# Branch hints on eleven loops, a larger DMA share of the transposes, and a clearing pass in smaller pieces, in a one-core attention and deformable-convolution kernel

## The reference

```python
# layer 0: group norm (32 groups), q/k/v, full attention over the 4096 pixels, projection, residual
h = group_norm(x, norm_w, norm_b)
qkv = einsum('bchw,dc->bdhw', h, qkv_w) + qkv_b
q, k, v = split(qkv.reshape(B, 3 * C, N), 3, axis=1)
attn = softmax(einsum('bcn,bcm->bnm', q, k) * C ** -0.5, axis=-1)
out = einsum('bnm,bcm->bcn', attn, v).reshape(B, C, H, W)
x = x + einsum('bchw,dc->bdhw', out, proj_w) + proj_b
# layer 1: conv 3x3, batch norm, relu; offsets by a second conv; deformable 3x3 conv; batch norm; residual, relu
out = relu(batchnorm(conv2d(x, w1), g1, b1))
offsets = conv2d(out, w_off) + b_off          # 18 offsets a pixel
out = batchnorm(deform_conv(out, offsets, w2), g2, b2)
return relu(out + x)
```

## Time and profile before

| | |
|---|---|
| three timed runs | 2494.53, 2494.78, 2497.68 us, median 2494.78 |
| the profiled execution | 2493.83 us, of which 2491.7 us lie between the first and the last instruction (the span) |
| busy: PE, DVE, ACT, POOL | 2315.7, 1855.8, 1795.1, 1310.9 us (93, 74, 72, 53% of the span) |
| attention, up to | about 1597 us |
| conv1, up to | about 1739 us |
| offset stage, up to | about 1872 us |
| sampling stage, up to | about 2440 us |

### The profile page before, as it was taken

How to read it: one execution, slowest core, us unless ns; L and a number is a source line. 1 busy time by engine, 2 the same in 40 slices (tenths; PEclk the granted TensorE clock), 3 DMA queues, 4 the chain that set the end, 5 groups by cost and what they waited for, 6 DMA issues and landing times.

```text
span 2491.7 us, 73903 instructions
## 1 busy us (share of the span) xinstructions
PE 2315.7 (93%) x27053; PEld 1877.2 (75%) x27053; DVE 1855.8 (74%) x3901; ACT 1795.1 (72%) x2963; POOL 1310.9 (53%) x1067
## 2 busy tenths in 40 slices
PE   5999999999999999999999999799877999899992
PEld 3777777777777777777777777588447999899992
DVE  6778777778877777877777777587666877777875
ACT  5778888878888888888888888532556766666754
POOL 4557545555545555544555555663116665556650
PEclk9999999999999999999999999899898999999996
DMA  3878887778787877877777777771224433333336
GB/s 108 166 144 147 141 162 140 147 149 146 145 159 133 150 145 145 150 129 129 149 147 146 148 146 148 192 235 59 66 71 133 124 113 113 111 111 117 115 95 270
DMA packets 917462, 345.25 MB, mean 139 GB/s; under 512 B 844256, under 2 KB 904160, under 8 KB 909024
## 3 DMA queue, kind: packets, MB, share of 16 engines
q1 hardware_dynamic: 917216, 341.87, 63.6%
HBM read 98.76 MB, written 41.68 MB: 56 GB/s over the span
## 4 chain that ended last, share of the span: by engine, by line
PE 75%; issue 9%; POOL 7%; DVE 4%; DMA 3%; ACT 1%; SPq 1%; POOLq 0%; DVEq 0%; ACTq 0%
PE psum L1041 14%; PE psum L1042 14%; PE psum L1043 14%; POOL probs_split L363 7%; PE psum L1080 7%; PE psum L1082 7%; PE psum L1081 7%; PE psum L1222 5%; PE psum L1066 3%; DMA probsT_dma<-probs_split 1%; PE psum L1195 1%; DMA final<-x_scratch 1%; DVE padded_hi L946 0%; PE psum L1120 0%; PE psum L1203 0%
## 5 line engine op out<-in xcount | busy, mean ns | idle before, releaser
L363 POOL TENSOR_TENSOR probs_split<-probs,probs_split 128x768 f16<-128x768 f32 x512 | 841.8, 1644 | 697.0 <-ACT probs_split L512 696.8
L711 DVE TENSOR_REDUCE neg_max<-psum 128x1 f32<-128x1024 f32 x512 | 626.6, 1224 | 333.0 <-PE psum L1043 332.8
L509 ACT ACTIVATE probs<-psum,exp_bias 128x1024 f32<-128x1024 f32 x512 | 570.2, 1114 | 220.2 <-DVE exp_bias L713 215.6
L1080 PE MATMUL psum<-vT_hi,probsT_dma 128*128 128x129 f16 x3072 | 549.6, 221 | 4.1 <-DMA probsT_dma<-probs_split 4.1
L1082 PE MATMUL psum<-vT_hi,probsT_dma 128*128 128x129 f16 x3072 | 549.5, 219 | 0.0
L1081 PE MATMUL psum<-vT_lo,probsT_dma 128*128 128x128 f16 x3072 | 549.4, 218 | 0.0
L512 ACT ACTIVATE probs_split<-probs 128x768 f16<-128x768 f32 x512 | 431.7, 843 | 22.8 <-ACT probs L509 1.0
L455 POOL TENSOR_TENSOR interp<-row_hats,col_hats 128x360 f32<-128x360 f32 x384 | 294.4, 795 | 219.6 <-PE psum L1222 214.7
L1041 PE MATMUL psum<-k_hi,q_hi 128*128 128x512 f16 x1024 | 387.8, 379 | 3.9 <-DVE q_lo L827 2.4
L1042 PE MATMUL psum<-k_lo,q_hi 128*128 128x512 f16 x1024 | 388.1, 379 | 0.0
L1043 PE MATMUL psum<-k_hi,q_lo 128*128 128x512 f16 x1024 | 388.1, 379 | 0.0
(11 more groups left out here) (181 smaller groups left out, 5532.1 us busy)
## 6 DMA issues: line engine op xcount, KB each, us to landing
xt_windows<-xt_scratch SPq DMA_DIRECT2D x192, 320.0 KB
xt_scratch<-zeros_f SPq DMA_DIRECT2D x28, 576.0 KB, 4.4
probsT_dma<-probs_split SPq DMA_TRANSPOSE x512, 3.7
x_residual<-x SPq DMA_DIRECT2D x128, 64.0 KB, 2.6
x_scratch<-x_out SPq DMA_DIRECT2D x128, 64.0 KB, 2.4
x_rows<-x_scratch SPq DMA_DIRECT2D x32, 256.0 KB, 3.4
xt_scratch<-xt_stage SPq DMA_DIRECT2D x128, 64.0 KB
final<-x_scratch SPq DMA_DIRECT2D x16, 512.0 KB, 10.7
```

What stands on the lines that cost most here:

```text
L363: po.tensor_tensor(PH[:, j, 1, :], P[:, j, 0:DW], PH[:, j, 0, :], ALU.subtract).then_inc(s["pl"], 1)
L509: act.activation(P[:, j, :], sc, ACT.Exp, bias=NB[:, par, j:j + 1]).then_inc(s["exp"], 1)
L711: ve.tensor_reduce(NM[:, par, j:j + 1], sc, AX.X, ALU.max, negate=True).then_inc(s["mx"], 1)
L1080: pe.matmul(dst, th, Vh[:, p, v, 0:129], start=n == 0, stop=False)
```

## The change

Three parts, made together.

1. **Loop hints, and clearing by blocks.** Eleven of the loops of layer 1 become `repeat(...)`, which is the same `Fori` with `hint_back_edge=True`: the first instruction of every iteration is a branch prefetch hint for the branch that closes the loop. These are conv1, the offset stage and the loop over halves on PE, DVE and ACT, and conv1 and the loop over halves on POOL. The attention loops, the loop over passes (one pass here) and SP's loops stay as they are. POOL clears `Y` with 32 memsets of 512 columns, each after ACT has read that block, in place of four of 4096.
2. **Key tiles.** In chunks 1 and 3 of each tile seven key tiles go by DMA and one by PE; in chunks 0 and 2 it stays at six and two. Each chunk has its own buffers.
3. **Late constants.** The columns from 454 on are loaded into a tile `CL` of layer 1's memory, by a DMA that SP issues after the conv1 loop, in place of the load at the start. The operation that makes `offset_high` from them moves from ahead of the first batch norm to behind it, and waits for the load.

```diff
-DT = 6
-DW = 128 * DT
+DT = (6, 7, 6, 7)
...
-        CN = sb_in(ctx, "constants", [128, K_ALL], F32)
+        CN = sb_in(ctx, "constants", [128, K_LO], F32)
...
+        CL = sb_in(l1, "late_constants", [128, K_ALL - K_LO], F32)
...
+        def repeat(eng, start, end):
+            return nc.Fori(start, end, engines=[eng.engine], hint_back_edge=True)
...
+            sp.dma_start(CL[:, :], consts[:, K_LO:K_ALL]).then_inc(s_kl, 16)
             sp.wait_ge(s_zf, 16 * 28)
...
-                    po.tensor_tensor(PH[:, j, 1, :], P[:, j, 0:DW], PH[:, j, 0, :], ALU.subtract).then_inc(s["pl"], 1)
+                    po.tensor_tensor(PH[j][:, 1, :], P[:, j, 0:128 * DT[j]], PH[j][:, 0, :], ALU.subtract).then_inc(s["pl"], 1)
...
-            for b in range(B):
-                after(po, "hA", (b + 1) * NCH)
-                po.memset(Y[:, b, :], 0.0).then_inc(s["fz"], 1)
+            for m in range(B * NCH):
+                after(po, "hA", m + 1)
+                po.memset(Y[:, m // NCH, 512 * (m % NCH):512 * (m % NCH) + 512], 0.0).then_inc(s["fz"], 1)
...
-                    act.activation(PH[:, j, 0, :], P[:, j, 0:DW], ACT.Copy).then_inc(s["ph"], 1)
+                    act.activation(PH[j][:, 0, :], P[:, j, 0:128 * DT[j]], ACT.Copy).then_inc(s["ph"], 1)
...
-            link(ve.tensor_scalar(HIGH[:, :, :], low, float(HH + 1), None, ALU.add))
             after(ve, "bs", B * NCH)
             norm(L1_VAR1, 10, vec(V_G1), vec(V_B1), 1)
             assert lstep[0] == L1_AB1
+            ve.wait_ge(s_kl, 16)
+            link(ve.tensor_scalar(HIGH[:, :, :], low, float(HH + 1), None, ALU.add))
...
-                for m in range(KT - DT):
-                    last = pe.transpose(PS[:, bank, 128 * m:128 * m + 128], P[:, j, DW + 128 * m:DW + 128 * m + 128], ident)
+                for m in range(DT[j], KT):
+                    at = 128 * (m - DT[j])
+                    last = pe.transpose(PS[:, bank, at:at + 128], P[:, j, 128 * m:128 * m + 128], ident)
                 last.then_inc(s["T"], 1)
...
-                with pe.Fori(1, NHALF) as h:
+                with repeat(pe, 1, NHALF) as h:
                     half_image(h, range(HALF), False)
```

More of the change, by code:

```diff
@@ L132, in build @@
         P = sb_in(l0, "probs", [128, CPT, CH], F32)
[L133 to L136, removed]
+        PH = [sb_in(l0, f"probs_split{j}", [128, 2, 128 * d], F16) for j, d in enumerate(DT)]
+        PDT = [sb_in(l0, f"probsT_dma{j}", [128, 2, d, 128], F16) for j, d in enumerate(DT)]
+        PTh = [sb_in(l0, f"probsT_hi{j}", [128, KT - d, 128], F16) for j, d in enumerate(DT)]
+        PTl = [sb_in(l0, f"probsT_lo{j}", [128, KT - d, 128], F16) for j, d in enumerate(DT)]
         ACC = sb_in(l0, "values_sum", [128, 2, VW], F32)
@@ L195, in build @@
         s_k = sem("constants_loaded")
+        s_kl = sem("late_constants_loaded")
         s_zf = sem("zero_rows_stored")
@@ L419, in conv1_in @@
                 po.tensor_tensor(VF[:, rb % 4, 3, :, :], ends[1][:, 1], ends[1][:, 0], ALU.subtract).then_inc(s["vf"], 1)
-            with po.Fori(0, B) as b:
+            with repeat(po, 0, B) as b:
                 for rb in range(NCH):
@@ L470, in _ @@
                     distances(n * NHALF, 0, 0, w)
-                with po.Fori(0, NHALF // 2 - 1) as u:
+                with repeat(po, 0, NHALF // 2 - 1) as u:
                     half_image(u * 2, 0, False)
@@ L501, in unit @@
                     after(act, "av", U - 5)
-                    act.activation(PTh[:, (j + 2) % 4, :, :].rearrange("p m q -> p (m q)"), PS[:, 4 + j % 2, 0:CH - DW],
+                    k = (j + 2) % 4
+                    act.activation(PTh[k][:, :, :].rearrange("p m q -> p (m q)"), PS[:, 4 + j % 2, 0:CH - 128 * DT[k]],
                                    ACT.Copy).then_inc(s["hi"], 1)
@@ L568, in _ @@
             conv1_image(0, True)
-            with act.Fori(1, B) as b:
+            with repeat(act, 1, B) as b:
                 conv1_image(b, False)
@@ L662, in half_image @@
                                 sampled(q - 1, (g + 1) % 2, i)
-                act.activation(SM[:, 32:34], CN[:, bass.ds((n + first_pass) * 2 + K_SH, 2)], ACT.Copy).then_inc(s["sh"], 1)
+                act.activation(SM[:, 32:34], CL[:, bass.ds((n + first_pass) * 2 + (K_SH - K_LO), 2)], ACT.Copy).then_inc(s["sh"], 1)
                 after(act, "sh", n + 1)
@@ L668, in _ @@
                 half_image(0, 0, True, False)
-                with act.Fori(0, NHALF // 2 - 1) as u:
+                with repeat(act, 0, NHALF // 2 - 1) as u:
                     half_image(u * 2 + 1, 1, False, False)
@@ L698, in _ @@
             boff = WF[:, W_BOFF:W_BOFF + NOFF][:, None, :].to_broadcast([128, GPI, NOFF])
-            low = CN[:, K_LO:K_SH].rearrange("p (q k) -> p q k", q=GPI)
+            low = CL[:, 0:K_SH - K_LO].rearrange("p (q k) -> p q k", q=GPI)
             ve.wait_ge(s_wh, 1)
@@ L888, in _ @@
             conv1_image(0, True)
-            with ve.Fori(1, B) as b:
+            with repeat(ve, 1, B) as b:
                 conv1_image(b, False)
@@ L967, in _ @@
             l1(ve.tensor_scalar(SM[0:1, 30:31], SM[0:1, 29:30], REACH, None, ALU.is_gt))
-            l1(ve.scalar_tensor_tensor(CNT[0:1, :], CN[0:1, K_CA:K_CB], SM[0:1, 30:31], CN[0:1, K_CB:K_ALL], ALU.mult, ALU.add))
+            l1(ve.scalar_tensor_tensor(CNT[0:1, :], CL[0:1, K_CA - K_LO:K_CB - K_LO], SM[0:1, 30:31], CL[0:1, K_CB - K_LO:K_ALL - K_LO], ALU.mult, ALU.add))
             assert lstep[0] == L1_FLAG
-            after(ve, "fz", B)
+            after(ve, "fz", B * NCH)
             npass = ve.value_load(CNT[0:1, 0:1], min_val=1, max_val=PASSES)
@@ L1023, in _ @@
                 half_image(0, range(HALF), True)
-                with ve.Fori(1, NHALF) as h:
+                with repeat(ve, 1, NHALF) as h:
                     half_image(h, range(HALF), False)
@@ L1159, in _ @@
             after(pe, "wg", 14)
-            with pe.Fori(0, B) as b:
+            with repeat(pe, 0, B) as b:
                 for rb in range(NCH):
@@ L1206, in _ @@
             offset_image(0, range(NCH), True)
-            with pe.Fori(1, B) as b:
+            with repeat(pe, 1, B) as b:
                 offset_image(b, range(NCH), False)
```

14 lines of the change are left out of this document (7 added, 7 removed).

## The result

| | before | after |
|---|---|---|
| median of the runs, us | 2494.66 (4 runs, 2493.39 to 2497.68) | 2452.97 (4 runs, 2450.76 to 2454.09) |
| span of the profiled execution, us | 2491.7 | 2452.0 |
| mean granted clock of TensorE | 0.970 | 0.973 |

The ratio is 0.983, with a 95% interval of 0.9813 to 0.9847: the change saves 41.7 us, where the prediction said 72.7. The measured time lies 6 us above the range given (2408 to 2447).

The account below looks back on a forecast made before the run. PE was taken to bound attention, conv1 and sampling, apart from the sampling loop's edges. From 2493.83 us, -28.0 + 1.5 - 40.7 - 5 - 0.5 = -72.7 gave 2421.1; predicted 2422, range 2408 to 2447.

Parts of the forecast that it names:

- Key tiles: Attention: 256 fewer f32 transposes on PE, -28.0 us, and +1.5 us for DMA waits beside the image loads.
- Late constants: Before the batch norm: `offset_high` leaves the path and lies behind ACT's first activation, -0.5 us.
- I take 0.5 us left at each edge: PE's sampling loop: hints leave 0.5 us at each of six back edges, -43.7 + 3.0 = -40.7 us.
- The price of the edges: PE's sampling loop: idle time and half-clock spells at its six back edges cost 43.7 us.
- The nearest rows: Back edges of PE's shorter loops, within 100 us of conv1 without idle time, cited because no row showed a hinted edge.
- signs of being wrong: "Issue" waits staying at L1230, `probsT_dma` waits growing beyond 6 us, or the offset stage longer than before.
- The hint does not reach PE's stop: Rival at the sampling loop's edges: hint too late in the queue, or another cause of the stop; 2463 us, chance 0.13.
- The stop moves: Rival: PE's edge is free, but ACT, DVE or POOL wait for code, some 3 us each time; 2440 us, chance 0.08.
- the rival in which the transposing DMA becomes the pace: Rival in the attention: transposing DMA sets the pace, so the 28 us do not come; 2450 us, chance 0.04.
- Clearing by blocks: Offset stage: -7.6 us of DVE copies held by memsets, +3 for slower copies, taken as -5, range -10 to +4.

Follow-up runs that it names:

- slot 64: Changed kernel with the head of PE's sampling loop placed at slot 64 of a 256-instruction block; 2447.37 us, ratio 0.9805.
- slot 136: Changed kernel with the head of PE's sampling loop at slot 136 of a 256-instruction block; 2433.72 us with that loop's hint, 2460.90 us without.

## Why the prediction was wrong

**The hints: the step that failed.** "I take 0.5 us left at each edge" gave -40.7; the sampling stage gave -11.4. The price of the edges was near (43.7 forecast, 40.2 measured by writing the loop out on the kernel before, and 42.1 from the changed kernel with no hints, 2469.35, to the written-out one with none, 2427.21, of which 39.0 lie in the sampling stage). What was wrong is what a hint brings. Three things were taken for granted. First, that a hinted target is there in time wherever the branch stands; with the branch early in its block (slot 64) stops of 1.6 to 4.5 us remain, and the kernel before with hints and the one with six tiles stop in the same way. Second, that the target's first block is all that is late; the second is late as well, when the head stands near its block's end (the changed kernel). Third, that a loop's exit stays free; with a hint it stops, in the changed kernel 3.4 us behind the sampling loop. The nearest rows that I bounded it by, PE's shorter loops with no idle time, were no evidence: in conv1 of the kernel before no packet ran on q8 between 1641 and 1756 us, in which time the loop turned three times, so its target never had to be fetched. Two of the prediction's own signs of being wrong came: "issue" waits stayed at L1230 (11.2 us, where under 4 was forecast), and the waits for `probsT_dma` went just over 6 us.

**The rivals.** "The hint does not reach PE's stop" had 0.13 and gave 2463. The measured time lay between it and the forecast: the hint reaches a part of the stop, which depends on where in its block the head happens to fall. No rival was about the place of the code, though the 16 KB packets were read as the cause of the stop. "The stop moves" to ACT, DVE or POOL did not come with the change: with PE's code straight and the others' loops hinted, PE is busy 416.2 of 420 us. It is not an empty rival: on the kernel before, where ACT's loop has no hint, it showed as two waits of PE of 4.4 us together.

**Key tiles: right.** Forecast -28.0 + 1.5; conv1 begins 24.0 us earlier, and undoing the part alone costs 25.2. The pace is the 11.40 us forecast. The waits on the transposed tiles have grown by 2.1 us (4.1 to 6.2). The rival in which the transposing DMA becomes the pace fell, even at seven tiles in each chunk.

**Clearing by blocks: right in sum.** Forecast -5. The part alone, with the hints in place, is worth 6.9 us of time and 7.6 of the stage; from the kernel before to the changed one with no hints the stage goes from 125.61 to 121.57, -4.0. These are single executions, and they differ by some us without a reason in the code: the stage takes 125.61 in the kernel before and 128.25 with only the sampling loop written out. Copies of 0.75 us against 0.8 forecast. The memsets are 0.53 us, a little over the 0.5 assumed.

**Late constants: right, and too small to be shown apart.** `offset_high` runs for 0.46 us at 1720.04, and conv1 to the offset stage is 0.3 us shorter.

## What to carry to other kernels

When PE stops at a loop's edge with "issue", the block structure of its code sets what a hint can give: the target's block must be asked for in time, and so must the block behind it, and in this kernel, with a body of eight blocks, each wanted some 4 to 6 us of work ahead of it. Write the hot loop out where it runs only a few times; here that was one line, 27 us better than the hint as placed and 8 better than the hint at the best of the places tried. If it has to be a loop, set the head near the middle of a block (the best of the places tried here), and look again after every edit ahead of it, since an edit elsewhere moves the head. Hint or write out the other engines' loops as well: once PE's stop is gone, theirs can show.

## What the runs showed of the hardware

- PE goes on 2.6 to 3.6 us after the start of the packet that brings the missing block, at all edges with a stop ahead of the first transpose of the kernels with slot 64, slot 136 with and without the hint, and the hints on the kernel before; inside an iteration of the changed kernel it is 2.5 to 2.9 us. The rest of a stop is the time until the packet starts.
- PE repeats the attention's loop of two tiles (552 instructions, the sequencer's included) without a packet on q8, but not the loop of one half image (some 2040).
- The hints of all eleven loops are worth 5.4 us on the kernel before and about 12 on the changed one (16.4, of which some 4.5 are not theirs); the hint of PE's sampling loop alone is worth 27.2 with its head at slot 136. The stops show the place of the code as the difference.
- A hinted loop can stop PE shortly behind its exit: 2.5 to 3.1 us at L1193, 3.4 us at L1050. The kernels with no hint on these loops lack both, but so do some hinted ones: slot 64 has none behind the sampling loop, and six or seven tiles everywhere none at L1193. It fits a fetch of the hinted block in place of the next one in order, which was not measured by itself.
- With slot 64 the nine transposes behind the stops of 1.6 to 2.9 us took 1.2 us, and behind those of 3.3 and 4.5 us 2.17. Without the hint at slot 136 they took 2.17 behind one of 2.9 us too. Part of what a shorter stop saves is therefore the clock.
- With 128x896 tiles the POOL subtraction takes 1.89 us against 1.92 in proportion, and the transposing DMA lands after 4.0 us (median) against 3.7 with six tiles, with its longest landing at 11.1.
